# Row maxima of the first image's attention scores: two groups of four heads on four banks, with the low parts of k computed ahead of them

## What is computed

```python
ch = c // NUM_HEADS                      # 16 channels a head
q, k, v = (qkv[:, :ch], qkv[:, ch:2 * ch], qkv[:, 2 * ch:])
w = jnp.einsum('bct,bcs->bts', q * scale, k * scale)
w = jax.nn.softmax(w.astype(jnp.float32), axis=-1).astype(qkv.dtype)
h = jnp.einsum('bts,bcs->bct', w, v).reshape(b, c, T)
```

## Time and profile before

| | |
|---|---|
| median of three runs | 530.28 us (529.22 to 533.23) |
| profiled execution, its own time | 526.66 us |
| its span, first to last instruction | 524.9 us |
| around the span | 1.8 us |
| PE busy | 455.3 us, 87% of the span |
| DVE busy | 351.0 us, 67% |
| ACT busy | 263.0 us, 50% |
| POOL busy | 136.0 us, 26% |
| one pass of the loop (pairs 2 to 5) | 47.4 us |

### The profile page before, as it was taken

The page is one execution under the profiler, slowest core; times in us unless marked ns, Lnnn a source line. Parts: engine busy times, 40 slices in busy tenths (PEclk is TensorE's granted clock), DMA queues, the critical chain, the costliest instruction groups (busy, mean ns, idle before and its releaser), DMA issues.

```text
span 524.9 us, 10106 instructions
## 1 busy us (share of the span) xinstructions
PE 455.3 (87%) x3522; PEld 354.0 (67%) x3522; DVE 351.0 (67%) x895; ACT 263.0 (50%) x654; POOL 136.0 (26%) x161
## 2 busy tenths in 40 slices
PE   4286786889999999999999999989988998785995
PEld 3163564467777768776776877677676788784885
DVE  1416856686769677877867786687466345675996
ACT  3321764555555364645555554535534514994540
POOL 6220375152104102210221131021111012503662
PEclk9996798979999999999999999999997999996999
DMA  5000111100000000000000000000000000004111
GB/s 218 20 8 15 38 34 30 55 21 22 1 1 22 21 1 20 20 0 0 20 20 0 0 20 0 1 21 2 0 4 19 1 22 2 0 1 160 42 56 64
DMA packets 9486, 13.15 MB, mean 25 GB/s; under 512 B 496, under 2 KB 8816, under 8 KB 9328
## 3 DMA queue, kind: packets, MB, share of 16 engines
q1 hardware_dynamic: 9456, 12.76, 7.2%
HBM read 8.56 MB, written 4.19 MB: 24 GB/s over the span
## 4 chain that ended last, share of the span: by engine, by line
PE 56%; DVE 20%; ACT 9%; issue 8%; POOL 4%; DMA 2%; DVEq 1%; SPq 0%; ACTq 0%; POOLq 0%
PE bank L1199 7%; PE bank L1312 5%; PE bank L1201 5%; PE bank L1200 5%; PE bank L1394 5%; PE bank L1368 4%; PE bank L1366 2%; PE bank L1344 2%; DVE nmax L992 2%; PE bank L1217 2%; PE bank L1422 2%; PE bank L1381 2%; ACT x L798 2%; DVE even L892 2%; DMA w_stage<-convs 1%
## 5 line engine op out<-in xcount | busy, mean ns | idle before, releaser
L1199 PE MATMUL bank<-win,w_hi 128*128 128x256 f32 x384 | 121.6, 317 | 12.4 <-DVE win L1145 5.9
L1201 PE MATMUL bank<-win,w_lo 128*128 128x256 f32 x384 | 109.1, 284 | 0.0
L1200 PE MATMUL bank<-win,w_hi 128*128 128x256 f32 x384 | 109.1, 284 | 0.0
L740 ACT ACTIVATE prob<-bank 128x512 f32<-128x512 f32 x128 | 69.6, 597 | 75.3 <-PE bank L1366 74.5
L992 DVE TENSOR_REDUCE nmax<-bank 128x2 f32<-128x512 f32 x128 | 85.2, 683 | 18.5 <-PE bank L1344 18.1
L1199 PEld LDWEIGHTS bank<-win,w_hi 128*128 128x128 f32 x384 | 73.5, 191 | 23.7 <-issue 10.8
L1200 PEld LDWEIGHTS bank<-win,w_hi 128*128 128x128 f32 x384 | 73.7, 192 | 0.5
L1201 PEld LDWEIGHTS bank<-win,w_lo 128*128 128x128 f32 x384 | 73.5, 191 | 0.0
L517 POOL TENSOR_TENSOR first<-first 128x256 f32<-128x256 f32 x24 | 17.7, 737 | 163.7 <-ACT first L629 163.7
L1368 PE MATMUL bank<-qk 32*128 32x256 f32 x256 | 41.3, 339 | 4.4 <-ACT prob L740 3.9
L1368 PEld LDWEIGHTS bank<-qk 32*128 32x128 f32 x256 | 24.8, 191 | 18.1 <-issue 5.6
(11 more groups left out here) (235 smaller groups left out, 924.3 us busy)
## 6 DMA issues: line engine op xcount, KB each, us to landing
w_stage<-convs SPq DMA_DIRECT2D x4, 576.0 KB, 3.8
x_in<-x SPq DMA_DIRECT2D x8, 256.0 KB, 2.6
out<-x_pair SPq DMA_DIRECT2D x8, 256.0 KB, 2.2
q<-out SPq DMA_DIRECT2D x1, 2048.0 KB, 8.2
out<-v SPq DMA_DIRECT2D x8, 256.0 KB, 2.1
cst<-small SPq DMA_DIRECT2D x1, 1708.0 KB, 8.7
cst<-small SPq DMA_DIRECT2D x1, 253.5 KB, 3.0
```

The lines of the kernel that those rows point to most:

```text
L740: act.activation(prob[:, x // 4 % 2, x % 4, :, :], bank[ST_BANK[x % 2]][:, :], ACT.Exp, scale=L2_SCALE).then_inc(st_exp, 1)
L1199: mm(dst, hi, x_hi, start=(row == 0), stop=False)
L1200: mm(dst, hi, x_lo, start=False, stop=False)
L1201: return mm(dst, lo, x_hi, start=False, stop=(row == KH - 1))
```

## The change

The first image's scores are now issued in two groups of four heads, `scores_group(j, 0, 4)` at the end of slot 1 and `scores_group(j, 4, 4)` at the end of slot 5, each on four banks: 6, 5, 3 and 4. A group is 8 products: one of each head for the first half of the rows, then one of each for the second half. Since banks 3 and 4 hold k's projection until its remainders are made, DVE issues both remainders at the head of the pair, before slot 0, and the first group waits for them (`qk_low`). DVE's row maxima of the first image move to slots 2 (heads 0, 1), 3 (2, 3), 6 (4, 5) and 7 (6, 7). The second image keeps its pairs of heads, banks and slots. Nothing is computed more or less often.

```diff
-K_LOW_SLOTS, V_SLOT, HEADS_SLOT, PROJECT_SLOT, ONES_SLOT = (3, 4), 3, 4, 5, 5
+QUAD_SLOTS, V_SLOT, HEADS_SLOT, PROJECT_SLOT, ONES_SLOT = (1, 5), 3, 4, 5, 5
+MAX_SLOTS = {2: (0, 1), 3: (2, 3), 6: (4, 5), 7: (6, 7)}
...
         def s_bank(n):
-            if n % 2 == 0:
-                return S2_BANK
-            return O_BANK if n < HEADS else S_BANK
+            if n < HEADS:
+                return (S2_BANK, O_BANK, *ST_BANK)[n % 4]
+            return S_BANK if n % 2 else S2_BANK
...
+                qk_low_parts(j, "k")
                 for s in range(SLOTS):
...
-                    if s < 2 * HEADS:
-                        row_max(j, s)
-                    if s in K_LOW_SLOTS:
-                        qk_low_parts(j, "k", (K_LOW_SLOTS.index(s),))
+                    for n in MAX_SLOTS.get(s, (s,) if HEADS <= s < 2 * HEADS else ()):
+                        row_max(j, n)
...
+                elif s_bank(n) in ST_BANK:
+                    pe.wait_ge(qk_low, 4 * j + 2 * QUADS)
...
-            def scores_pair(j, n):
-                for x in (n, n + 1):
+            def scores_group(j, n, size):
+                for x in range(n, n + size):
                     scores(j, x)
                 for k in range(CH):
-                    for x in (n, n + 1):
+                    for x in range(n, n + size):
...
-                    if n < HEADS and s % 2 == 0:
-                        scores_pair(j, s)
+                    if 0 <= n < HEADS and s % 2 == 0:
+                        scores_group(j, s, 2)
...
+                    if s in QUAD_SLOTS:
+                        scores_group(j, 4 * QUAD_SLOTS.index(s), 4)
                     if n in (0, HEADS):
                         scores_t_pair(j, n)
```

## The result

The kernel after takes **540.59 us** (median of 4, 539.40 to 545.98) against 531.02 (529.22 to 533.23) for the kernel before: ratio 1.0199, 95% interval [1.0132, 1.0267]. That is slower, and above the predicted range of 526.5 to 538.5.

A forecast was written before the change was run, and what follows sets the result against it. It took PE to bound the kernel on average and DVE the stretch from the `xht` copy to `logit1`; pair losses 0 + 1.2 + 1.3 + 0.2 + 0 = 2.7 us on 530.28 gave 533.0 us, range 526.5 to 538.5.

The forecast's parts named there:

- What leaves PE: Scores leaving slots 0 and 4 free 0.63 and 0.43 us on PE; the loop's copy of `xht` comes 0.87 earlier.
- What DVE gets behind it: Between the copy of `xht` and `maxima_t` DVE takes four row maxima instead of two: 3.54 us becomes 4.74.
- `maxima_t` 0.33 later, wait 1.4: In each of pairs 2 to 5 `maxima_t` starts 0.33 us later; PE's wait there grows from 0.23 to 1.4.
- A group costs what a pair costs, four side by side: Four heads' score products run beside each other on PE, so a group in a former pair's place costs nothing more.
- Two by two: Rival: a group's four heads run in twos, delaying `xht` in pairs 1 to 6; 1.2 to 2.6 us on top, chance 0.13.
- The wait for the remainders costs nothing in the loop: The first group waits for both k remainders, which in the loop are through about 0.7 us before PE arrives: nothing.
- Pair 6, 0.1 to 0.2: Without x stages the full 1.06 us gain reaches the copy, against 1.20 more on DVE: 0.1 to 0.2 us slower.
- Pair 0, 0 with 1.2 as the upper end: `maxima_t` comes about 0.8 us later, but PE waits 0.98 for POOL there: no loss, at most 1.2.
- Pair 1, 1.2: With no convolution in these slots there is no gain; `maxima_t` comes 1.20 us later, 0.6 as lower end.
- the waits at 391 stand with others: Argument against the clock falling in the loop: the idle stretch at 391.35 to 398.18, followed by half clock, had other waits too.
- the rival in which it falls: PE's longer wait before `maxima_t` lowers the granted clock in pairs 2 to 5: up to 13.6 us on top, chance 0.12.
- The rival's check, "if the clock row of a pass falls below 1.00": Sign that the forecast is wrong: a loop pass whose granted clock falls below the forecast 1.00.

The follow-up runs named there:

- e1: The unedited changed kernel again on another chip, against the kernel before: 540.37 us against 531.30, ratio 1.0218.
- e2: The change in pairs 2 to 5 (the loop) alone, other pairs as before, against the kernel before: 537.53 us against 531.30, ratio 1.0165.
- e3: The change in the written-out pairs 0, 1, 6 and 7 alone, loop as before, against the kernel before: 535.19 us against 531.30, ratio 1.0043.
- e7: Kernel before plus two unused row maxima on DVE ahead of the eighth in pairs 2 to 5, against the kernel before: 541.21 us against 531.58, ratio 1.0147.
- e9: The change in pairs 2 to 7, pairs 0 and 1 as before, against the kernel before: 537.23 us against 532.17, ratio 1.0106.
- e5: The change in pairs 2 to 5 with two constant matmuls filling PE's wait before `maxima_t`, against the kernel before: 534.90 us against 531.58, ratio 1.005.
- e6: The whole change with two constant matmuls before every pair's first `maxima_t`, against the kernel before: 538.02 us against 531.58, ratio 1.0119.
- e12: Second group ahead of `xht` in pairs 2 to 7, plus constant matmuls in three pair 0 waits, against the kernel before: 529.96 us against 532.26, ratio 0.9964.

## Why the prediction was wrong

- *What leaves PE* (0.63 and 0.43, 0.87 at the copy of `xht`): right, 0.88.
- *What DVE gets behind it* (3.54 becomes 4.74): right. 19.34 - 14.60 = 4.74.
- *`maxima_t` 0.33 later, wait 1.4*: right, 0.32 and 1.43. The pass is 47.74, predicted 47.75.
- *A group costs what a pair costs, four side by side*: right; 8 products 0.51, a pair's four 0.50. (The place in slot 0 is worth 0.65 by the prediction's own working, which wrote 0.63.) "Two by two" falls. The Trainium skill's 3.07 times for four row tiles ("TensorE: Matmul & The Clock Gate", "Measured speedup vs the span model") would have had the group some 0.1 longer (an estimate from that page); 0.51 against 0.50 doesn't show that.
- *The wait for the remainders costs nothing in the loop*: right, no wait stands before line 1346 at 259.47.
- *Pair 6, 0.1 to 0.2*: e1's stretch is 18.33 against 18.19, 0.14. *Pair 7, 0*: 0.1 less.
- *Pair 0, 0 with 1.2 as the upper end*: 0 to 0.4. `maxima_t` came 0.9 later, and most of that was absorbed behind it: e1's pair 0 takes 48.57, e2's, in the order before and with as much half-clock time, 48.56.
- *Pair 1, 1.2*: 1.6, read between e3 and e2 at equal half clock. Mis-sized by 0.4. What the 0.4 beyond the two counted row maxima is, I haven't separated.
- *"Against: the waits at 391 stand with others", and "in the loop the clock never fell"*: **this is the step that failed**. The sum took the granted clock as unchanged in all pairs, and the rival in which it falls had a chance of 0.12 and was thought of for the loop alone. What the runs showed in its place: the median execution of e1 has 21.8 us more at half clock than before. The loop's stretch with the wait is as idle as the one at 391.35 (5.30 of 6.82 busy against 5.25 of 6.83), which the prediction itself had named, and that could have been worked out then: 1.2 us more idle time within 6.8. e2, e7 and e9 show one fall in the loop each, 13.65 us long and not 6.82, so it costs 5.3 and not 3.4. Outside the loop pair 1, with 6.8 us at half clock before, holds 20.7 and 21.0 such microseconds in the two profiles of the change; e2, e7 and e9, whose pair 1 is in the order before, hold 10.2 to 10.4 there, so in these profiles some 10 of the 14 us of growth come with the change.
- *The rival's check, "if the clock row of a pass falls below 1.00"*: in the two profiles of the change none did. The executions say more than the profiles here: their mean clock was 0.926 to 0.949 after.

Of the 9.1 us in e1, then, about 3 are the rows, and the other 6 go with the lower clock. That an idle PE brings on falls is shown for the loop (e2, e7 and e9 have one, e5 hasn't, and its executions have most of the clock back). But the full change's own two profiles have none in the loop. For pair 1, where they have theirs, it is only likely: the 13.65 us stand behind waits of 2.21 and 2.02, and filling the wait removed them in one profile, but e3 has 6.8 behind the same wait, and e6's time did not follow. For pairs 0 and 6 the falls stand in unchanged pairs as well and are not shown to be the change's. So what lowers the clock of the full change's executions, and by how much in which pair, is in part open. And why equal passes with equal waits fall in one pair and not in the next stays open.

## What to carry to other kernels

Before moving work from a busy TensorE to another engine's list, add up that list between the two points at which TensorE looks at it; the time saved on TensorE comes back as a wait there. Price such a wait at its length and, beside that, give a stretch of half clock behind it a chance of its own where the trace shows a fall behind a stretch as idle; equal stretches here kept the clock in some passes and lost it in others, so it is a chance and not a rule. Before a fall is put down to a change, look for it in stretches that the change doesn't touch, in several profiles. Compare kernels whose times differ by 1% with a dozen executions each and look at their mean clocks; a better place for the moved work (ahead of the transfer that DVE waits for) can remove the wait (here from 1.43 to 0.23).

## What the runs showed of the hardware

- One wait of 1.40 to 1.42 us, with PE busy 5.26 to 5.35 of 6.8 to 6.9 us around it, was followed by 13.6 us at 1.2 GHz in three kernels of different order (e2, e7, e9), and in each of them in one of four equal passes only; in the two profiles of the full change it was followed by none.
- Products of constants whose result nothing reads, put into the wait, left 4.6 us more at half clock than before instead of 12.9 (e5 against e2), and in pair 0 they took away a fall that all other profiles have (e12: 14.92 us became 11.97 with more products in it).
- Four products of 32 rows each run beside one another without a visible cost: 8 take 0.51, 4 take 0.50. What such a group adds between products of 128 rows hardly grows with the number of heads: 0.43 to 0.65 for two, 0.44 and 0.63 for four.
- One kernel's executions spread over 526.8 to 536.3 us on one chip (before, 23 executions), the longest mostly at the lowest mean clock (four of five at 0.938), and this is more than all the rows of this change together. Falls outside the loop come and go between profiles in pairs whose code is the same (pair 0: 6.83 or 13.65 us at its end; pair 6: none or 6.83).
